# Layer norm statistics for two groups at once in a macaron block kernel (one core)

## What is computed

```python
def _layernorm(x, axis=-1, eps=1e-05):
    m = jnp.mean(x, axis=axis, keepdims=True)
    v = jnp.var(x, axis=axis, keepdims=True)
    return (x - m) / jnp.sqrt(v + eps)

x = x + 0.5 * _L0_ffn_ref(_layernorm(x), router_w, wg, wu, wd)   # 8 experts, top 2, capacity 1.25 N / 8
x = x + _L0_attn_ref(_layernorm(x), Wq, bq, Wk, bk, Wv, bv, Wo, bo)
x = x + 0.5 * _L0_ffn_ref(_layernorm(x), router_w, wg, wu, wd)
```

## Times and profile before

| what | value |
|---|---|
| median of 3 runs | 1757.87 us |
| profiled execution | 1756.62 us |
| its span | 1754.9 us |
| input stage A, first statistics to the start of the second routing block | 6.2 to 74.97 us |
| input stage B, the same | 965.66 to 1046.17 us |
| VectorE busy over the span | 1124.3 us (64%) |
| GpSimd busy over the span | 756.9 us (43%) |

### The profile page before, as it was taken

The page is one execution under the profiler, slowest core; times in us unless marked ns, Lnnn a source line. Parts: engine busy times, 40 slices in busy tenths (PEclk is TensorE's granted clock), DMA queues, the critical chain, the costliest instruction groups (busy, mean ns, idle before and its releaser), DMA issues.

```text
span 1754.9 us, 40276 instructions
## 1 busy us (share of the span) xinstructions
PE 1590.5 (91%) x14526; PEld 1254.2 (71%) x14526; DVE 1124.3 (64%) x2523; ACT 885.6 (50%) x1624; POOL 756.9 (43%) x611
## 2 busy tenths in 40 slices
PE   5649999999999999986799664999999999999997
PEld 4536878787877778764688653687878787777876
DVE  7898484848566674626788788746374645556461
ACT  5645454544444444526676564445454544545452
POOL 7403525343443425035776650452534444342503
PEclk9999999999999999997999765999999999999999
DMA  8754616252433435037777460452615243443402
GB/s 266 246 164 125 130 43 129 57 129 52 110 68 94 76 86 85 7 39 184 163 154 160 138 229 6 125 102 65 135 50 117 69 111 67 96 76 87 85 7 31
DMA packets 274528, 182.73 MB, mean 104 GB/s; under 512 B 174219, under 2 KB 261141, under 8 KB 274453
## 3 DMA queue, kind: packets, MB, share of 16 engines
q1 hardware_dynamic: 243732, 139.11, 29.2%
q0 software_dynamic: 30720, 42.62, 15.5%
HBM read 89.66 MB, written 55.05 MB: 82 GB/s over the span
## 4 chain that ended last, share of the span: by engine, by line
PE 79%; DVE 10%; ACT 3%; issue 3%; DMA 3%; POOL 2%; SPq 0%; DVEq 0%; POOLq 0%; ACTq 0%
PE bank L1618 48%; PE bank L1634 24%; ACT xt L747 2%; PE bank L1596 1%; PE bank L1564 1%; PE bank L1675 1%; DVE bank L335 1%; DMA xs<-x_d 1%; DVE xn L1025 1%; DVE xn L1114 1%; POOL rows L527 1%; PE bank L1687 1%; PE bank L1506 1%; PE bank L1707 1%; PE bank L1517 1%
## 5 line engine op out<-in xcount | busy, mean ns | idle before, releaser
L1618 PE MATMUL bank<-xT,rows 128*128 128x320 f16 x3072 | 500.5, 299 | 1.0 <-DVE w_u L1004 1.0
L1618 PE MATMUL bank<-xT,w_u 128*128 128x320 f16 x3072 | 500.8, 299 | 0.0
L1241 DVE SCALAR_TENSOR_TENSOR unit_buf<-bank,sc_cur,unit_buf 128x320 f32<-128x320 f32 x512 | 281.6, 550 | 326.5 <-PE bank L1618 318.5
L796 ACT ACTIVATE unit_buf<-bank,sc_cur 128x320 f32<-128x320 f32 x512 | 269.7, 527 | 375.9 <-PE bank L1618 375.0
L1634 PE MATMUL bank<-w_d,xs 128*128 128x256 f16 x3840 | 421.9, 273 | 0.0
L1634 PEld LDWEIGHTS bank<-w_d,xs 128*128 128x128 f16 x3840 | 375.2, 98 | 43.9
L1618 PEld LDWEIGHTS bank<-xT,w_u 128*128 128x128 f16 x3072 | 300.6, 98 | 116.7
L1618 PEld LDWEIGHTS bank<-xT,rows 128*128 128x128 f16 x3072 | 291.6, 98 | 109.5 <-issue 2.0
L457 POOL DMA_INDIRECT gat<-rows_d,id_next x160 | 184.4, 1152 | 312.0 <-issue 254.7
L1247 DVE TENSOR_TENSOR xs<-unit_buf,xs 128x320 f16<-128x320 f32 x512 | 247.1, 483 | 2.2
L802 ACT ACTIVATE xs<-unit_buf 128x320 f16<-128x320 f32 x512 | 235.6, 460 | 10.4 <-DVE unit_buf L1241 10.4
(11 more groups left out here) (235 smaller groups left out, 1623.5 us busy)
## 6 DMA issues: line engine op xcount, KB each, us to landing
rows_d<-rows SPq DMA_DIRECT2D x32, 512.0 KB, 3.7
raw_gu<-in_L_ffn_wg SPq DMA_DIRECT2D x16, 1024.0 KB, 6.8
raw_gu<-in_L_ffn_wu SPq DMA_DIRECT2D x16, 1024.0 KB, 8.7
raw_d<-in_L_ffn_wd SPq DMA_DIRECT2D x16, 1024.0 KB, 5.3
x_d<-xs SPq DMA_DIRECT2D x1, 8192.0 KB, 32.9
out_x<-xs SPq DMA_DIRECT2D x16, 512.0 KB, 3.6
xs<-in_L_attn_x SPq DMA_DIRECT2D x7, 1024.0 KB, 7.5
xs<-x_d SPq DMA_DIRECT2D x6, 1024.0 KB, 6.2
```

The costliest lines, as they stand in the source:

```text
L796: act.activation(act_s[:, u % 2, :], bank[u % 2][:, 0:CW], ACT.Silu, scale=sc_cur[:, 3:4]).then_inc(S.s_ready, 1)
L1241: dve.scalar_tensor_tensor(h32[:, u % HB, :], bank[2 + u % 2][:, 0:CW], sc_cur[:, 4:5], act_s[:, u % 2, :], mult, mult).then_inc(S.h32_rea ...
L1618: mm = pe.matmul(bank[2 * m + u % 2][:, 0:CW], wgu[m][:, w, k, f * P:(f + 1) * P], xT[:, a * KD + k, c * CW:(c + 1) * CW], start=(j == 0 a ...
```

## The change

`moments`, `mean_r` and `rstd` get four slots instead of two, so that two steps' groups have places of their own; `slots(i)` are the two of step i. The statistics of both groups of step i+1 are taken at the start of the first half of step i (`turn(i, 0)`); one variance, one power and one means then cover both groups (8 columns instead of 4). The second half of a step has norms alone. Groups 0 and 1 stay single: group 1's variance and power follow its own statistics, and in step 0 the statistics of groups 2 and 3 are both taken in the second half. On GpSimd the power of step i+1 stands before `low` of group 2i, from step 1 on; in step 0 it stands between the two `low`. The last step of VectorE has no statistics and no second means.

```diff
--- before.py
+++ after.py
@@ -91,10 +91,10 @@
         rows32 = rows[:, :, :, :].rearrange("p b t c -> p (b t c)").bitcast(f32).rearrange("p (b t c) -> p b t c", b=RING, t=G4)
         xn = sb("xn", [P, 2, G4, D], f32)
         xt2 = sb("xt2", [P, 2, 2, 2 * KD, P], f16)
-        moments = bank[1][:, 256:256 + 6 * G4].rearrange("p (r g s) -> p r g s", r=2, g=G4)
+        moments = bank[1][:, 256:256 + 12 * G4].rearrange("p (r g s) -> p r g s", r=4, g=G4)
         top_mask = bank[5][:, :].rearrange("p (t e) -> p t e", e=E)
-        mean_r = bank[1][:, 288:288 + 2 * G4].rearrange("p (r g) -> p r g", r=2)
-        rstd = sb("rstd", [P, 2, G4], f32)
+        mean_r = bank[1][:, 304:304 + 4 * G4].rearrange("p (r g) -> p r g", r=4)
+        rstd = sb("rstd", [P, 4, G4], f32)
         nmean = sb("nmean", [P, 2, G4], f32)
         ident16 = sb("ident16", [P, P], f16)
         ident = sb("ident", [P, P], f32)
@@ -338,6 +338,10 @@
 
             return v.tensor_scalar(rstd[:, r, part], moments[:, r, part, 2], XSCALE ** -2 / D, EPS * XSCALE ** -2, mult, add)
 
+        def slots(i):
+
+            return slice(2 * (i % 2), 2 * (i % 2) + 2)
+
         def batches(eng, body):
 
             body(-1, range(QUADS))
@@ -475,9 +479,10 @@
                 pool.sem_inc(S.landed, 1)
 
             def ffn(S, dst, head, beside):
-                def power(q, r):
-                    pool.wait_ge(S.stat_ready, q + 1)
-                    pool.tensor_tensor(rstd[:, r, :], rstd[:, r, :], mhalf[:, :], ALU.pow).then_inc(S.rstd_ready, 1)
+                def power(n, part):
+                    pool.wait_ge(S.stat_ready, n)
+                    pool.tensor_tensor(rstd[:, part, :], rstd[:, part, :], bc(mhalf[:, :], 1, part.stop - part.start),
+                                       ALU.pow).then_inc(S.rstd_ready, 1)
 
                 def low(q, r):
                     pool.wait_ge(S.hi_ready, q + 1)
@@ -486,20 +491,22 @@
                                        sub).then_inc(S.lo_ready, 1)
 
                 def step(i, beside):
-                    power(2 * i + 1, 1)
+                    if i:
+                        power(i + 3, slots(i + 1))
                     low(2 * i, 0)
                     beside(2 * i)
-                    power(2 * i + 2, 0)
+                    if i == 0:
+                        power(3, slots(1))
                     low(2 * i + 1, 1)
                     beside(2 * i + 1)
 
-                power(0, 0)
+                power(1, slice(0, 1))
                 beside(-1)
+                power(2, slice(1, 2))
                 for i in range(head):
                     step(i, beside)
                 for i in range(head, STEPS - 1):
                     step(i, nothing)
-                power(2 * STEPS - 1, 1)
                 low(2 * STEPS - 2, 0)
                 low(2 * STEPS - 1, 1)
                 for j in range(RING):
@@ -1007,35 +1014,49 @@
             def ffn_in(S, ch, wait_x, head, beside):
                 def stats(i, r):
 
-                    t = i * PAIR + r * G4
                     wait_x(i, r)
                     for pair in range(2):
-                        ch.mark(two_moments(dve, r, pair, t))
-
-                def variance(r):
-                    variance_of(dve, r).then_inc(S.stat_ready, 1)
-
-                def means(i, r):
-                    dve.wait_ge(S.rstd_ready, 2 * i + r + 1)
-                    ch.mark(dve.tensor_tensor(mean_r[:, r, :], moments[:, r, :, 1], rstd[:, r, :], mult))
+                        ch.mark(two_moments(dve, slots(i).start + r, pair, i * PAIR + r * G4))
+
+                def variance(part):
+                    dve.tensor_scalar(rstd[:, part, :], moments[:, part, :, 2], XSCALE ** -2 / D, EPS * XSCALE ** -2, mult,
+                                      add).then_inc(S.stat_ready, 1)
+
+                def means(n, part):
+                    dve.wait_ge(S.rstd_ready, n)
+                    ch.mark(dve.tensor_tensor(mean_r[:, part, :], moments[:, part, :, 1], rstd[:, part, :], mult))
+                    ch.wait()
+                    settle(dve)
 
                 def norm(i, r, tile):
+                    at = slots(i).start + r
                     if tile == 0:
                         dve.wait_ge(S.lo_ready, 2 * i + r + 1)
                     ins = dve.scalar_tensor_tensor(xn[:, r, tile, :], tiles(xs, i * PAIR + r * G4 + tile, 1)[:, 0],
-                                                   rstd[:, r, tile:tile + 1],
-                                                   mean_r[:, r, tile:tile + 1].to_broadcast([P, D]), mult, sub)
+                                                   rstd[:, at, tile:tile + 1],
+                                                   mean_r[:, at, tile:tile + 1].to_broadcast([P, D]), mult, sub)
                     if tile == G4 - 1:
                         ins.then_inc(S.xn_ready, 1)
 
                 def turn(i, r):
-                    n = r ^ 1
-                    stats(i + r, n)
-                    means(i, r)
-                    ch.wait()
-                    settle(dve)
+                    last = i == STEPS - 1
+                    if i == 0:
+                        if r == 0:
+                            stats(0, 1)
+                            ch.wait()
+                            variance(slice(1, 2))
+                        else:
+                            stats(1, 0)
+                            stats(1, 1)
+                        means(r + 1, slice(r, r + 1))
+                    elif r == 0:
+                        if not last:
+                            stats(i + 1, 0)
+                            stats(i + 1, 1)
+                        means(i + 2, slots(i))
                     norm(i, r, 0)
-                    variance(n)
+                    if r == (i == 0) and not last:
+                        variance(slots(i + 1))
                     norm(i, r, 1)
                     norm(i, r, 2)
                     norm(i, r, 3)
@@ -1048,17 +1069,12 @@
 
                 stats(0, 0)
                 ch.wait()
-                variance(0)
+                variance(slice(0, 1))
                 beside(0)
                 for i in range(head):
                     step(i, beside)
-                for i in range(head, STEPS - 1):
+                for i in range(head, STEPS):
                     step(i, nothing)
-                turn(STEPS - 1, 0)
-                means(STEPS - 1, 1)
-                ch.wait()
-                for tile in range(G4):
-                    norm(STEPS - 1, 1, tile)
 
             def route(S, ch):
```

## The result

| | before | changed |
|---|---|---|
| median | 1757.86 us (13 runs, 1755.74 to 1758.89) | 1762.01 us (13 runs, 1760.4 to 1767.08) |
| ratio, 95% interval | | 1.0027 [1.0020, 1.0034] |
| profiled execution, its span | 1756.62, 1754.9 us | 1762.97, 1761.2 us |
| stage A, start of the second routing block | 74.97 us | 76.49 us |
| stage B, first statistics to the second routing block | 80.51 us | 85.33 us |

The change costs 4.15 us between the medians, 0.24% (the ratio of the table gives 0.27%). The two profiled executions differ by more, 6.3 us of span: 1.52 in stage A, 4.82 in stage B, and under 0.1 us between the two stages (890.7 and 890.6 us) and behind them (708.7 and 708.8). The forecast was 1760.4 with 1755.4 to 1763.6, so the time is inside the range but 1.6 us above the forecast.

What follows compares the result with a forecast made beforehand. The prediction took the ring of ScalarE, TensorE and GpSimd as the bound in both FFNs' input stages. +1.2 (first), +1.25 (second) and +0.1 (steady) gave +2.5 us, 1760.4 us on the median; range 1755.4 to 1763.6.

Steps and rivals of the forecast that it cites:

- ring of ScalarE, TensorE and GpSimd: Steady steps of the first FFN's input stage: these engines set the 7.11 us period; VectorE has slack, saving it nothing.
- VectorE sets the pace: Rival, both FFNs' input stages: each step saves 0.38 us, 4.9 us over 13 steps; 1753.0 us, chance 0.07.
- start is made up: Rival: slack in the ring makes up the 2.3 us late start, only the ends count; 1755.6 us, chance 0.13.
- The start of stage A: Start of the first FFN's input stage: uncovered extra statistics make group 3's high part 2.3 us late, and it stays.
- Its end: End of the first FFN's input stage: group 15's norm no longer waits for its power, giving back 1.15 us.
- The power: GpSimd's power of 128x8, estimated at 1.61 us from 0.15 us a column and 0.41 fixed.
- the steady term of 0.1 us: Even low part slightly late, at most 0.05 us a period; 0.1 us over seven periods of both FFNs' input stages.
- Stage B: Second FFN's input stage: 2.4 us later at attention's woven-in last product, less 1.15 at the end; 1.25 us later.
- TensorE waits for it and has its transposes of group 1 behind it in its queue: Second FFN's input stage: VectorE's line 1394 comes 2.4 us later, delaying TensorE and all behind it by 2.4 us.
- more delay in stage B: Rival: six statistics may push a finish, 1.2 us, and the same in the first FFN's input stage; 1762.8 us, chance 0.12.
- long power rival: Rival: an eight-column power of 2.02 us costs 0.4 us a period, 2.9 us over seven; 1763.3 us, chance 0.18.
- H + 3.3: Steady step, H an odd group's high-part start: the next odd norm may begin here; even norms complete at H + 9.4.

Runs made afterwards that it cites:

- run 2: The change in the second FFN's input stage alone, the first FFN's in the old order; 1760.75 us, ratio 1.0022 to the kernel before.
- run 7: The changed kernel with the routing's first maximum written to TensorE's bank memory, nothing else; 1761.17 us, ratio 1.0025 to the kernel before.
- run 3: The changed kernel with six unused matmuls ahead of attention's last product in the second FFN's input stage; 1760.27 us, ratio 1.0021 to the kernel before.
- run 8: The changed kernel with a second, unused 128x4 power behind each power of eight columns; 1765.45 us, ratio 1.0050 to the kernel before.
- run 4: The kernel before, with groups paired only from step 5 of the second FFN's input stage; 1758.53 us, ratio 1.0011 to the kernel before.
- run 5: The kernel before, with groups 14 and 15 alone paired in both FFNs' input stages; 1756.51 us, ratio 0.9999 to the kernel before.
- run 1: The change in the first FFN's input stage alone, the second's in the old order; 1757.97 us, ratio 1.0007 to the kernel before.
- run 6: The kernel before, with groups 14 and 15 alone paired and the routing's first maximum in bank memory; 1754.66 us, ratio 0.9989 to the kernel before.

## Why the prediction was right, and where it was short

**The bound** was read rightly: ring of ScalarE, TensorE and GpSimd, period 7.11 before and 7.10 after, VectorE's saved operations worth nothing. The "VectorE sets the pace" and "start is made up" rivals fell with that; after five periods the high part of group 13 is 2.24 us late (62.09 against 59.85), as group 3's was (2.26, 26.57 against 24.31).

**The start of stage A**: +2.3 forecast, +2.26 measured; each time on the way was within 0.1 us. **Its end**: -1.15 forecast, -1.18 measured. **The power**: 1.61 forecast from a line through two forms, 1.63 measured; the steady term of 0.1 us didn't show. By the rate per element of the Trainium skill (GPSIMD Engine Reference, performance versus the Vector engine) an estimate is 1.02 us; the measurement decides.

**Not in the sum: the routing's subtraction.** I took it that an earlier norm of group 15 is an earlier routing. It moved the subtraction under a low part of GpSimd, 0.45 us in each stage. The rows for it were in view: at 66.46 us before, this subtraction just missed the low parts.

**Stage B: +1.25 forecast, +4.82 in the profile, about +3.8 by run 2's time.** By its terms:

| term | forecast | measured |
|---|---|---|
| line 1394 behind two more pairs of statistics | +2.4 | +2.36 |
| product and transposes of group 1 at the low clock | 0 | +1.34 (m less line 1410's place: 6.94 us in run 7, 5.60 before) |
| the clock still low in the next half step | 0 | +0.95 (26.19 against run 7's 25.24) |
| between that reduction and the high part of group 10 | 0 | +0.89 (33.96 against 33.07 us) |
| norm of group 15 (from the high part of group 10 to the routing: 15.63 against 16.81 us) | -1.15 | -1.18 |
| the routing's subtraction | 0 | +0.46 |
| sum | +1.25 | +4.82 |

The step that fell short is "TensorE waits for it and has its transposes of group 1 behind it in its queue": I counted the wait and left the durations behind it as they were. In runs 3, 7 and 8 the wait carried the product past the moment at which the clock fell; in the changed kernel's and run 2's profiles the clock hadn't risen at all, and why it came as late as 40 us there is open. The fourth term is VectorE's: the four statistics in one piece ahead of the norm of group 8 (1013.86, 2.51 us) make its high part wait 1.65 us for VectorE, where it waited 0.79 before. That was the "more delay in stage B" rival's first half (six statistics push a finish). Its time, 1762.8, is nearest to the result, but its 1.2 us in stage A wasn't there, and the clock, 2.3 of the 3.6 us that were missing in the profile, was in none of the cases. That the time is inside the range is partly luck: its upper 3.2 us were room for a long power and more delay in both stages, and the clock used them.

The clock also explains why the profiles differ by 6.3 us and the medians by 4.15. Before's profiled execution had the product at the high clock and was 1.24 us below its median; runs 4 and 5 show that the same order can also get the low clock. The changed kernel's profiled execution was one in which the clock came back late (+0.95), and 0.96 above its median. How often each happens was not counted, and the mean granted clock of a whole execution (0.954 to 0.961 over the 13 of the changed kernel and the 33 of before beside runs 1 to 4) is too coarse for it.

**The long power rival** was priced twice too high: 0.4 us a period at a power of 2.02. By run 8's rows half of it would have lengthened the period, an estimated 1.4 us over seven periods instead of 2.9. Its threshold, 1.65 us, fits both: at 1.63 the copies start without a wait, and in run 8, at 2.66, they were ready 0.98 us late. Two slips in the working changed nothing: the chances of a slower result add up to 0.29 and not 0.28, and the terms behind H + 3.3 to H + 9.24 and not 9.4; in the changed kernel those norms were complete at H + 9.3.

## What to carry to other kernels

Fewer and wider operations on an engine that isn't the bound brought nothing here, and doing two groups' work at once moves the second group's share ahead of whatever stood between them: pay attention to the start of a pipeline and to woven-in work, where nothing covers it. Take such a change only where it frees an order that the bound waits for, here the last pair (run 6, 0.1% faster and only with the maximum in TensorE's bank memory), and look at what the freed work then runs into. When a step is moved on an engine that TensorE waits for, look up the granted clock at that place and price the work behind the wait at both levels.

## What the runs showed of the hardware

- A power on GpSimd over 128x8 took 1.63 us beside 1.01 for 128x4 and 0.71 for 128x2: 0.15 us a column and about 0.4 fixed.
- A VectorE subtraction of 128x384 with both operands in SBUF took 1.01 us (changed kernel), 1.14 (run 5) and 1.67 (run 8) instead of 0.56 while GpSimd was at work, and ended 0.41 to 0.42 us behind GpSimd's operation; with one operand in TensorE's bank memory it took 0.55.
- The same order of work got different clocks: four matmuls of 128x256 in f32 took 1.13 us in three profiles and 2.07 in two (before's order up to there), and the clock rose 14.6 to 15.1 us behind the stage's first statistics in the three and 20.3 and 20.1 in the two. The Trainium skill ("TensorE: Matmul & The Clock Gate", Part 1) calls the point at which the clock rises run-variable; these profiles agree.
- 22 unused matmuls at the high clock, ended at 979.74 us, didn't keep it for a product at 985.08 with 3.1 us of other work between them (1.07 + 1.11 + 2 x 0.46); the clock fell at about 985.3.
- Six unused matmuls of 128x512 that began at 983.03 us didn't hold the clock either (run 3): it fell at about 984.1, while they ran.
